# A macaron block on one core: the first feed-forward half written out in another order on VectorE, ScalarE, GpSimd and TensorE

## The reference

```python
x = x + 0.5 * ffn(_layernorm(x), W_up, W_gate, W_down)
x = x + attn(_layernorm(x), Wq, Wk, Wv, Wo, head_scale)
x = x + 0.5 * ffn(_layernorm(x), W_up, W_gate, W_down)

def ffn(x, W_up, W_gate, W_down):
    wu, wg, wd = (ternary_quant(w) for w in (W_up, W_gate, W_down))
    return (silu(x @ wu.T) * (x @ wg.T)) @ wd.T        # 256 -> 1024 -> 256

def ternary_quant(w):
    scale = mean(abs(w)) + 1e-8
    return clip(round(w / scale), -1, 1) * scale
```

## Time and profile before

| | |
|---|---|
| median of 3 runs | 1135.9 us (1135.78 to 1137.19) |
| profiled execution: its own time, its span | 1136.0 us, 1134.2 us |
| busy share: PE, DVE, ACT, POOL | 95%, 85%, 70%, 63% |
| chain that ended last, by engine | PE 70%, issue 10%, POOL 8%, DVE 7%, ACT 3%, DMA 1% |
| first feed-forward half | 0 to about 227 us |
| attention | about 227 to 962 us |
| second feed-forward half | to the end |

### The profile page before, as it was taken

How to read it: one execution, slowest core, us unless ns; L and a number is a source line. 1 busy time by engine, 2 the same in 40 slices (tenths; PEclk the granted TensorE clock), 3 DMA queues, 4 the chain that set the end, 5 groups by cost and what they waited for, 6 DMA issues and landing times.

```text
span 1134.2 us, 27100 instructions
## 1 busy us (share of the span) xinstructions
PE 1073.0 (95%) x8465; PEld 839.6 (74%) x8465; DVE 959.3 (85%) x2369; ACT 790.2 (70%) x1964; POOL 719.0 (63%) x886
## 2 busy tenths in 40 slices
PE   4697888979999999999999999999999998999998
PEld 2354555658888888888888888888888886555555
DVE  5787888699999999999999999999999997433433
ACT  4363665568878888878878788788787885554453
POOL 4653555567777777777777777777777773544443
PEclk9798999999999999999999999999999999999999
DMA  9421112134533443434344434334344344100101
GB/s 347 116 48 38 38 37 55 20 60 76 80 71 71 82 76 70 80 71 89 66 77 83 79 69 79 74 74 79 69 79 79 69 79 80 29 20 18 37 18 37
DMA packets 262130, 79.88 MB, mean 70 GB/s; under 512 B 249296, under 2 KB 260816, under 8 KB 261840
## 3 DMA queue, kind: packets, MB, share of 16 engines
q1 hardware_dynamic: 261664, 79.19, 33.8%
q10 hardware_dynamic: 432, 0.27, 0.1%
HBM read 12.85 MB, written 4.19 MB: 15 GB/s over the span
## 4 chain that ended last, share of the span: by engine, by line
PE 70%; issue 10%; POOL 8%; DVE 7%; ACT 3%; DMA 1%; DVEq 0%; POOLq 0%; ACTq 0%
PE bank L666 45%; PE bank L727 14%; POOL SCR L386 6%; PE bank L655 4%; PE bank L627 3%; PE bank L637 3%; DVE X L853 1%; DVE SCR L863 1%; ACT SCR L557 1%; DMA SCR<-ARENA 1%; ACT SCR L473 1%; DVE SCR L827 1%; DVE ARENA L1032 1%; ACT NHL L465 1%; POOL RSTD L373 1%
## 5 line engine op out<-in xcount | busy, mean ns | idle before, releaser
L414 POOL TENSOR_SCALAR SCR<-SCR,RI 128x128 f32<-128x128 f32 (+1 forms) x512 | 309.3, 604 | 44.0 <-DVE RI L1028 3.8
L399 POOL TENSOR_TENSOR SCR<-SCR 128x512 f32<-128x512 f32 x160 | 203.2, 1270 | 150.2 <-DVE SCR L993 148.9
L557 ACT ACTIVATE SCR<-bank,NM 128x128 f32<-128x128 f32 (+1 forms) x512 | 208.5, 419 | 125.4 <-DVE NM L1012 125.4
L386 POOL TENSOR_TENSOR SCR<-SCR 128x512 f16<-128x512 f32 x128 | 154.2, 1205 | 196.4 <-ACT SCR L479 196.2
L863 DVE SCALAR_TENSOR_TENSOR SCR<-SCR,CS,bank 128x512 f32<-128x512 f32 x128 | 95.3, 745 | 128.7 <-PE bank L637 90.4
L727 PE MATMUL bank<-SCR 128*128 128x128 f32 (+1 forms) x1024 | 193.2, 331 | 3.7 <-ACT SCR L557 3.7
L529 ACT COPY SCR<-bank 64x512 f32<-64x512 f32 x320 | 185.7, 580 | 13.8 <-PE bank L666 7.3
L1032 DVE TENSOR_TENSOR ARENA<-SCR,ARENA 128x768 f16<-128x768 f32 x128 | 187.8, 1467 | 4.3 <-ACT ARENA L564 3.4
L666 PE MATMUL bank<-WOH,ARENA 128*128 128x256 f16 x1024 | 188.5, 273 | 2.2 <-DVE ARENA L1023 1.3
L479 ACT CAST SCR<-SCR 128x512 f16<-128x512 f32 x128 | 79.1, 618 | 152.8 <-DVE SCR L863 102.9
L1012 DVE CUSTOM_DVE_ANT_0 bank<-bank,MASK,SCQ 128x128 f32<-128x128 f32 (+1 forms) x512 | 182.9, 417 | 0.8
(11 more groups left out here) (113 smaller groups left out, 1646.7 us busy)
## 6 DMA issues: line engine op xcount, KB each, us to landing
out<-X SPq DMA_DIRECT2D x7, 512.0 KB, 2.9
X<-in_x SPq DMA_DIRECT2D x1, 2560.0 KB, 10.4
ARENA<-in_wq SPq DMA_DIRECT2D x1, 2048.0 KB, 12.9
ARENA<-in_wo SPq DMA_DIRECT2D x1, 2048.0 KB, 18.1
SCR<-ARENA SPq DMA_TRANSPOSE x128, 3.6
X<-in_x SPq DMA_DIRECT2D x3, 512.0 KB, 9.6
X<-in_wu SPq DMA_DIRECT2D x1, 1024.0 KB, 6.8
X<-in_wg SPq DMA_DIRECT2D x1, 1024.0 KB, 9.0
```

Source lines behind the costliest of these rows:

```text
L386: gp.tensor_tensor(HL[:, f % 4, :], H32[:, f % 2, :], HH[:, f % 4, :], ALU.subtract).then_inc(s["hl_done"], 1)
L399: gp.tensor_tensor(dst, M1[:, m, :], M2[:, m, :], ALU.add).then_inc(add, 1)
L414: last = gp.tensor_scalar(EX[:, par, lo:hi], EX[:, par, lo:hi], RI[:, par, c:c + 1], PS, ALU.mult, ALU.mult)
L557: last = act.activation(EX[:, par, 384 * hh + lo:384 * hh + hi], SBK[hh][:, lo:hi], ACT.Exp, bias=NM[:, par, c:c + 1], scale=-1.0, accum_o ...
```

## The change

It rewrites the order of layer 0 and one wait of both layers:

- Jobs: tuples are now (f0, fc, fh, fl, q, tile), with norm_hi in fh and norm_lo in fl. Tiles 1 to 6 have stats in step 3, center and norm_hi in step 4 and norm_lo in step 5 for job 2n; stats in 6, center and norm_hi in 7 and norm_lo in step 0 of the next tile for job 2n+1. Tile 7 has the first of these only. Tile 0 has center 1, norm_hi 2, norm_lo 3.
- `residual` is written before stats in its step.
- All ternary compares are DVE's; GpSimd has none.
- The maxima move to tiles 1 to 3, CUT0 becomes 4, and the casts, one step earlier each, are in tiles 4 to 7. `scales()` is cut in two, `diagonal()` in step 6 and `scales()` in step 7 of tile 3.
- PE: 20 f32 matmuls of the identity before the first turn and 8 more before total(1) (`keep_warm`); total(1) ahead of the first up; `down` of step 0 waits for half of the residual at its start and for the rest before its third sub-block.

```diff
-        CUT0 = 3
+        CUT0 = 4
...
             if isinstance(n, int) and n == 0:
-                return [(-1, 2, 5, 1, 1)]
+                return [(-1, 1, 2, 3, 1, 1)]
             if isinstance(n, int) and n == TILES - 1:
-                return [(4, 5, 6, 2 * n, n - 1)]
-            return [(0, 1, 2, 2 * n, n + 1), (4, 5, 6, 2 * n + 1, n - 1)]
+                return [(3, 4, 4, 5, 2 * n, n - 1)]
+            return [(3, 4, 4, 5, 2 * n, n + 1), (6, 7, 7, FC, 2 * n + 1, n - 1)]
...
@@ scalar: ffn and weights @@
-                    for f0, _, ft, q, tile in jobs:
-                        if f == ft:
+                    for f0, _, fh, _, q, tile in jobs:
+                        if f == fh:
                             norm_hi(q, *turned_ahead(n, f0))
...
-                if not isinstance(n, int) and f in (1, 3, 4, 5):
+                if (not isinstance(n, int) or n >= CUT0) and f in (0, 2, 3, 4):
...
@@ tensor @@
+            def keep_warm(times):
+
+                for _ in range(times):
+                    pe.matmul(GB[1][:, 0:P], IDF[:, :], IDF[:, :], start=True, stop=True)
...
-                if making and f == 0:
-                    total(1)
...
                 if f == 0:
-                    wait(pe, s["x_done"], SUB * n)
+                    wait(pe, s["x_done"], SUB * n - SUB // 2 if not isinstance(n, int) or n > 0 else 0)
...
                 for sub in range(SUB):
+                    if f == 0 and sub == SUB // 2:
+                        wait(pe, s["x_done"], SUB * n)
...
             pe.wait_ge(consts, 5)
+            keep_warm(20)
             first_turn()
             total(0)
+            keep_warm(8)
+            total(1)
             ffn(0, 0, False)
...
@@ vector: ffn @@
-                    for f0, _, _, q, tile in jobs:
+                    if layer == 0 and f == 0 and (not isinstance(n, int) or n > 1):
+                        norm_lo(2 * n - 1)
+                    if f == LAG - 1 and prev:
+                        residual(layer, n - 1)
+                    for f0, fc, _, fl, q, tile in jobs:
                         if f == f0:
-                            if f0 == 4:
+                            if f0 == 6 or isinstance(n, int) and n == TILES - 1:
                                 wait_alone(ve, s["x_done"], SUB * n)
                             stats(q, tile)
-                    if f == LAG - 1 and prev:
-                        residual(layer, n - 1)
-                    for _, fc, ft, q, tile in jobs:
                         if f == fc:
                             center(q, tile)
-                        if f == ft + 1:
+                        if f == fl:
                             norm_lo(q)
...
@@ vector: weights @@
-                    maxima = {(0, 5): (1, 0), (0, 6): (2, 0), (0, 7): (0, 0), (1, 2): (0, 1), (1, 3): (0, 2), (1, 6): (0, 3),
-                              (1, 7): (3, 0), (2, 2): (3, 1), (2, 3): (3, 2), (2, 6): (3, 3)}
+                    maxima = {(1, 0): [(1, 0)], (1, 1): [(2, 0)], (1, 4): [(0, 1)], (1, 5): [(0, 0)], (2, 1): [(0, 2), (0, 3)], (2, 5): [(3, 0)],
+                              (3, 1): [(3, 1), (3, 2)], (3, 5): [(3, 3)]}
...
-                    if (n, f) == (2, 6):
+                    if (n, f) == (CUT0 - 1, 5):
...
-                    if (n, f) == (2, 7):
+                    if (n, f) == (CUT0 - 1, 6):
+                        diagonal()
+                    if (n, f) == (CUT0 - 1, 7):
                         scales()
-                elif f in (2, 4, 5, 6):
+                if (not isinstance(n, int) or n >= CUT0) and f in (1, 3, 4, 5):
...
+            def ternary_piece(i, q):
+
+                raw, t = quarter(i, q)
+                ve.tensor_scalar(t, raw, FNEG[:, i:i + 1], None, ALU.is_lt).then_inc(less, 1)
+                ve.wait_ge(less, ORDER.index((i, q)) + 1)
+                ve.scalar_tensor_tensor(t, raw, FHALF[:, i:i + 1], t, ALU.is_gt, ALU.subtract).then_inc(tern[i], 1)
```

More of the change, by code:

```diff
@@ L161, in program @@
         tern = [sem(f"ternary_ready{i}") for i in range(3)]
-        f_tot, f_sc, tern_a, less = (sem(n) for n in ("f_total", "f_scales", "tern_first_cmp", "tern_cmp"))
+        f_tot, f_sc, less = (sem(n) for n in ("f_total", "f_scales", "tern_cmp"))
         a_sc_dve = sem("a_scale_steps")
@@ L214, in program @@
                    4: [(1, 3)], 5: [(2, 2)], 6: [(2, 3)]}
-        LESS = {-1: [(0, 1), (1, 1)], 0: [(0, 2), (2, 0)], 1: [(1, 2), (0, 3)], 2: [(2, 1), (1, 3)], 3: [(2, 2)], 4: [(2, 3)]}
-        LESS_ORDER = [q for f in LESS for q in LESS[f]]
+        ORDER = [q for f in TERNARY for q in TERNARY[f]]
         def quarter(i, q):
@@ L243, in turned_ahead @@
                 return 0, 0
-            if f0 == 0 or isinstance(n, int) and n == TILES - 1:
-                return 1, n
-            return 0, n
+            return (1, n) if f0 == 3 else (0, n)
         def ends(b):
@@ L373, in rstd @@
                 gp.tensor_tensor(RSTD[:, :], VE[:, :], NEGHALF[:, :], ALU.pow).then_inc(ln_rs, 1)
[L375 to L380, removed]
             def ffn(layer, n, jobs):
@@ L386, in ffn @@
                     gp.tensor_tensor(HL[:, f % 4, :], H32[:, f % 2, :], HH[:, f % 4, :], ALU.subtract).then_inc(s["hl_done"], 1)
-                    if layer == 0 and isinstance(n, int) and n == 0 and f in LESS:
-                        compare(f)
-                    for f0, _, _, q, _ in jobs:
+                    for f0, _, _, _, q, _ in jobs:
                         if f == f0:
@@ L438, in _ @@
             rstd(0)
-            compare(-1)
             rstd(1)
@@ L495, in weights @@
                         act.mul(RO[:, h * D:(h + 1) * D], RO[:, h * D:(h + 1) * D], HS[:, h:h + 1]).then_inc(hs_mul, 1)
-                if not isinstance(n, int) and f in (1, 3, 4, 5):
+                if (not isinstance(n, int) or n >= CUT0) and f in (0, 2, 3, 4):
                     act.wait_ge(a_sc, 1)
-                    raw, hi, _, size, c = CUTS[(1, 3, 4, 5).index(f)]
+                    raw, hi, _, size, c = CUTS[(0, 2, 3, 4).index(f)]
                     cols = bass.ds((n - CUT0) * size, size)
@@ L681, in ffn @@
                         total(2)
-                    if layer == 0 and isinstance(n, int) and (n, f) == (2, 7):
+                    if layer == 0 and isinstance(n, int) and (n, f) == (CUT0 - 1, FC - 1):
                         largest()
@@ L887, in weights @@
                 if isinstance(n, int):
-                    maxima = {(0, 5): (1, 0), (0, 6): (2, 0), (0, 7): (0, 0), (1, 2): (0, 1), (1, 3): (0, 2), (1, 6): (0, 3),
-                              (1, 7): (3, 0), (2, 2): (3, 1), (2, 3): (3, 2), (2, 6): (3, 3)}
-                    if (n, f) in maxima:
-                        w, piece = maxima[n, f]
+                    maxima = {(1, 0): [(1, 0)], (1, 1): [(2, 0)], (1, 4): [(0, 1)], (1, 5): [(0, 0)], (2, 1): [(0, 2), (0, 3)], (2, 5): [(3, 0)],
+                              (3, 1): [(3, 1), (3, 2)], (3, 5): [(3, 3)]}
+                    for w, piece in maxima.get((n, f), ()):
                         ve.wait_ge(attn_raw, 64)
@@ L912, in ternary @@
             def ternary(f):
-                for i, q in TERNARY[f]:
-                    if f == -1:
+                if f == -1:
+                    for i in range(2):
                         ternary_scale(i)
[L917 to L925, removed]
+                        ternary_piece(i, 0)
+                        if i == 0:
+                            first_lo()
+                else:
+                    for i, q in TERNARY[f]:
+                        ternary_piece(i, q)
                 if f == 0:
                     ternary_scale(2)
+            def ternary_piece(i, q):
[3 more added lines that the diff above has]
+                ve.scalar_tensor_tensor(t, raw, FHALF[:, i:i + 1], t, ALU.is_gt, ALU.subtract).then_inc(tern[i], 1)
             def ternary_scale(i):
@@ L948, in ternary_scale, with diagonal @@
                     ve.wait_ge(f_sc, 7)
-            def scales():
+            def diagonal():
                 ve.wait_ge(a_turn, 1)
@@ L954, in scales @@
                 ve.tensor_scalar(AMD[:, :], IDF[:, 0:4], AMC[:, 0:1], None, ALU.mult).then_inc(a_diag, 1)
+            def scales():
                 ve.wait_ge(a_tot, 1)
@@ L975, in _ @@
             for n in range(CUT0):
-                if n > 0:
+                if 0 < n < 3:
                     ve.wait_ge(xin[n + 1], 16)
```

2 lines of the change are left out of this document (1 added, 1 removed).

## The result

The changed kernel takes 1142.6 us (median of 4 runs, 1142.33 to 1143.48) against 1136.1 for the kernel before on the same chip (1135.78 to 1137.19): ratio 1.0057, 95% interval 1.0040 to 1.0075. It is slower by 6.6 us; 1142.2 was predicted. The profiled span is 1140.5 us at a granted clock of 0.992 (the share of TensorE's full clock that the profile shows as granted), against 1134.2 at 0.989.

The account below looks back on a forecast made before the run. It took a chain from h to h over DVE and ACT to bound layer 0, not PE. Tile 0 -8.6, tiles 1 to 7 +17.0 and layer 1 -2.1 gave +6.3: 1142.2 us, range 1138 to 1147 (58%).

Parts of the forecast that it names:

- The chain bounds layer 0: Layer 0: a chain from h to h over DVE and ACT, 2.02 us without side work, sets the tile time, not PE.
- Center and norm_hi: Layer 0, 13 steps: norm_hi waits for center in the same step with silu queued behind it; 5.7 to 6.3 us each.
- Step 7: Second center step of a tile: rstd wait, center, norm_hi, silu and hand-overs add up to 5.7 us.
- step 4: First center step of a tile with casts: rstd wait, center, norm_hi, WOH, silu and hand-overs add up to 6.3 us.
- The rival in which silu does not wait for norm_hi: Center steps cost 3.9 us, some 2.1 less in 13 steps: -27 us, about 1115; chance 6%.
- the one in which center runs alone: Center misses HL in steps 4 and 7 and takes 1.35 us in 13 steps: -10.8 us, 1131.4; chance 12%.
- A loop tile: Layer 0 loop tiles: eight steps sum to 27.8 us against 24.07, 3.7 more per tile, 11.2 for three.
- The other tiles: Tiles 1, 2, 3 and 7 up to h of step 7: 29.3, 26.2, 26.7, 21.7 us; with loop tiles +17.0.
- Tile 0: Earlier first h (18.1) and all quarters on DVE bring tile 1's first h to 45.5: -8.6 us; bounds 43.3 and 52.
- The meetings: Tile 0: DVE work overlapping GpSimd's HL, counted as 2.2 us up to h of step 7.
- Layer 1: Residual wait at tile borders: waiting for half gains 0.3 us in each of 7 tiles, -2.1; bounds 0 and -4.4.
- The clock: PE pauses of 3.1 to 3.8 us in steps 4 and 7 lower its clock: 6% for 1145 to 1155, 2% beyond.

Follow-up runs that it names:

- silu-first kernel: The changed kernel with each job's norm_hi, except tile 0's, issued on ACT one step later, behind that step's silu and ahead of its HH copy: 1121.7 us, ratio 0.9867.

## Why the prediction was right

- **The chain bounds layer 0: right.** With PE's work unchanged, an instruction moved on ACT gave 21 us back, and the same one moved the other way cost 31.
- **Center and norm_hi: right.** Step 7 was put at 5.7 and measured 5.65, step 4 at 6.3 and 6.30. The rival in which silu does not wait for norm_hi falls by the 2.42 us that DVE stands for silu; the one in which center runs alone falls by the 2.22 and 2.21 that it took in the loop tiles.
- **A loop tile: 27.8 against 28.75 measured.** Seven steps came within 0.1. (The eight steps as listed add up to 27.9, and tile 7's to 21.8 instead of 21.7; both are rounding.) The term that was mis-sized is "5: h 0.66, norm_lo 1.12, WOL 1.2, so 3.0"; step 5 was 3.90. VectorE there, and HL on GpSimd:

```profile
170.78 1.22 DVE L833 TENSOR_TENSOR NHL<-SCR,NHL 128x1024 f16<-128x1024 f32 x1
171.92 2.18 DVE L905 SCALAR_TENSOR_TENSOR WOL<-ARENA,AFAC,WOH  x1
```

```profile
171.59 1.42 POOL L375 TENSOR_TENSOR SCR<-SCR 128x512 f16<-128x512 f32 x1 [5.08 <-ACT SCR L465]
```

  I had taken WOL's time from a step where it met nothing, though the prediction itself priced such a meeting at 0.96 in tile 0. HL starts about 1.5 after h, and norm_lo with WOL reaches over it. Four such steps (tiles 4 to 7) are 3.6 us. Here WOL, starting 0.33 after HL, took 0.91 longer than the 1.27 of the earlier trace rows, when HL had 1.09 of its 1.42 left.
- **The other tiles:** tile 1 28.93 (29.3), tile 2 26.04 (26.2), tile 3 26.40 (26.7), tile 7 to h7 22.45 (21.7, with the same missing 0.9 in step 5). Together 190.0 against 187.3, so +19.7 instead of +17.0.
- **Tile 0: -11.0 instead of -8.6.** Tile 1's first h at 43.16 lies just under the lower bound of 43.3, which was to hold if no meeting cost anything. Meetings did cost; what the sum had wrong is the price of a compare. Alone it took 0.48 (0.51 to the next start), not the 0.80 I counted, as the 0.77 of the earlier trace rows had stood beside GpSimd's own compare. Ten of them make 2.9. The first h came at 17.05, not 18.1, for the same reason: the shorter turning was already in the forecast, and with the compares on GpSimd the first h is at 18.04. That the early matmuls would bring the higher pace before the turning was my estimate, which no row of the kernel before shows; in the kernel after the turning took 1.06, without them 1.94. The meetings took 2.9 instead of 2.2, and they fell on the compares, not on the combines: three of the ten compares took 1.38, all ten combines 0.75. One such compare, and one that met nothing:

```profile
18.52 1.47 POOL L375 TENSOR_TENSOR SCR<-SCR 128x512 f16<-128x512 f32 x1
18.89 1.38 DVE L925 TENSOR_SCALAR TG<-X,FNEG 128x512 f16<-128x512 f32 x1
...
22.16 0.48 DVE L925 TENSOR_SCALAR TU<-X,FNEG 128x512 f16<-128x512 f32 x1
```

  By the runs the early job is worth 7.6, DVE's compares 1.3, the keep-warm 1.1. Taken back one at a time these sum to 10.0 of the 11.0. The other 1.0 is left to total(1) ahead of the up, the moved maxima and what the parts do together; none of it was tried singly.
- **Layer 1: right.** VectorE's residuals of the kernel after stand 20.80 apart instead of 21.11, and the part behind h7 shrank by 2.4 (2.1 predicted):

```profile
996.08 1.66 DVE L847 SCALAR_TENSOR_TENSOR X<-bank,CY,X 128x256 f32 x4 [0.18 <-PE bank L646]
...
1016.88 1.27 DVE L847 SCALAR_TENSOR_TENSOR X<-bank,CY,X 128x256 f32 x3 [0.18 <-PE bank L646]
```

- **The clock: the price was right, its place was not.** I put pauses of 3.1 to 3.8 us into the two center steps. In the loop tile the long silu of step 4 reaches PE as a pause of 0.85 only: from 163.06 to 169.30 PE has earlier groups to run. Its one long pause is for the turned columns: norm_lo ends at 172.00, behind the long step 4, and the columns are first used at 176.71:

```profile
170.14 1.04 PE L618 MATMUL bank<-XX,TU 128*128 x4 [0.85 <-ACT SCR L459]
...
176.71 1.88 PE L618 MATMUL bank<-XX,TU 128*128 x4 [3.79 <-DMA XX<-NHL]
```

  PE starts the tile at half pace (granted clock 0.56 from 176 to 178, 0.58 from 178 to 180), but step 7 lasts 5.65 anyway, and this is hidden. In the silu-first kernel the waits for turned columns in the loop are at most 2.5 us, and the matmuls behind this one run at 1.03:

```profile
163.19 1.03 PE L623 MATMUL bank<-XX,TU 128*128 x4 [2.55 <-DMA XX<-NHL]
```

- The total came out 0.4 us from the forecast because the misses cancel: 2.7 too little for tiles 1 to 7, against 2.4 too little gain in tile 0 and 0.3 in layer 1. That closeness is luck; the sums were good to about 2.5 us each. What was not tried is the residual in front of the statistics, or a plan with the steps of before, on the changed kernel.

## What to carry to other kernels

In an engine's in-order queue, an instruction that waits for another engine's work of the same step holds up everything behind it (in the changed kernel's center step norm_hi stood 2.20 us on ACT, and DVE then 2.42 for the silu behind it): put the instruction that the critical chain needs next (here silu) ahead of it. Here that gave back 0.2 to 0.3 us in two steps of a loop tile and was worth 21 us in all. A plan that spreads work evenly over one engine's steps must be read on every engine's queue: with the same order on VectorE tiles 1 to 7 take 190.0 us with norm_hi in front of silu and 169.1 behind it, against 170.3 before. (The silu-first kernel is 15 us faster than the one before in all, but 11 of these are tile 0's and 2 layer 1's.) Take a duration from a row whose neighbours on the other engines are those of the new place, not from the fastest row.

## What the runs showed of the hardware

- A DVE compare of 128x512 (f32 to f16) took 0.48 us with GpSimd idle, 0.77 and 0.84 beside a GpSimd compare, and 1.38 where it met HL (for instance at 18.89 in the kernel after). With the compares on DVE seven of the ten compares behind tile 0's first h so cost less than the row of before, and three cost more.
- The 28 keep-warm calls stand in the trace as 56 matmul records. The first 40 took 6.38 us: the first 15 started over 3.2 us (from 2.1 to 5.3), the last 23 over 2.4 (from 5.8 to 8.2), with the granted clock at 1.00 throughout. The first turning, 0.63 behind them, took 1.06 instead of the 1.94 without them.
- A pause of 5.81 us cost not only itself but three matmul groups at 1.9 instead of 1.03, in the 5 us behind it; h showed it in the second step behind the long one. After a pause of 2.55 us the groups ran at 1.03.
